# A projection phase in another order: its own PSUM region for queries and for keys, and the moments two images ahead

## What is computed

```
mu = jnp.mean(inputs, axis=-1, keepdims=True)
var = jnp.mean(jnp.square(inputs - mu), axis=-1, keepdims=True)
x = (inputs - mu) / jnp.sqrt(var + LN_EPS) * ln_gamma + ln_beta
q = (x @ Wq + bq).reshape(B, S, H, dh)
k = (x @ Wk + bk).reshape(B, S, H, dh)
v = (x @ Wv + bv).reshape(B, S, H, dh)
```

## Time and profile before

| What | us |
|---|---|
| Median of 3 runs | 4483.35 |
| Lowest and highest of them | 4482.82 and 4495.68 |
| The profiled execution, whole | 4445.29 |
| Its span in the profile | 4443.5 |
| The projection phase in it, first x load to first load of attention | 260.68 |

### The profile page before, as it was taken

One profiled execution on the slowest core, in us unless ns is written; L12 is line 12 of the kernel. 1 busy time (PEld: TensorE's weight loads), 2 busy tenths in 40 slices (PEclk: granted clock), 3 DMA queues, 4 the chain that ended last, 5 costly groups with the idle time before them and its releaser, 6 DMA issues. The chain is left out here.

```text
span 4443.5 us, 74057 instructions
## 1 busy us (share of the span) xinstructions
PE 3361.3 (76%) x26644; PEld 2596.9 (58%) x26644; DVE 2938.2 (66%) x5398; ACT 2246.5 (51%) x3488; POOL 653.8 (15%) x613
## 2 busy tenths in 40 slices
PE   5888888887565888888888888888754447777773
PEld 3665665664453666666666666666544435555552
DVE  7899989986342777777777777777644424444443
ACT  2454445453343766666666666666522224444440
POOL 1000000000110000000000000000077744444441
PEclk9999999999776999999999999999855568888885
DMA  2121322222357999999999999999733234444437
GB/s 78 59 109 66 115 110 79 98 106 106 140 213 239 368 369 358 374 357 374 355 379 352 380 359 358 356 373 373 272 101 128 71 114 156 152 156 154 150 137 303
DMA packets 281139, 988.62 MB, mean 222 GB/s; under 512 B 47796, under 2 KB 53824, under 8 KB 271734
## 3 DMA queue, kind: packets, MB, share of 16 engines
q1 hardware_dynamic: 263542, 950.62, 58.8%
q0 software_dynamic: 17280, 33.87, 2.1%
HBM read 494.69 MB, written 489.85 MB: 222 GB/s over the span
## 5 line engine op out<-in xcount | busy, mean ns | idle before, releaser
L1141 ACT ACTIVATE att_skewed<-att_skewed,att_neg_max 128x1024 f32<-128x1024 f32 x512 | 588.7, 1150 | 438.9 <-DVE att_neg_max L1201 438.9
L1272 PE MATMUL att_turn_ps<-att_ident,att_skewed 128*128 128x128 f32 x4096 | 579.6, 287 | 158.0 <-ACT att_skewed L1141 156.6
L1201 DVE CUSTOM_DVE_ANT_0 att_skewed<-att_score_ps,att_skewed 128x1024 f32<-128x1024 f32 x512 | 626.1, 1223 | 85.5 <-issue 73.5
L1272 PEld LDWEIGHTS att_turn_ps<-att_ident,att_skewed 128*128 128x128 f32 x4096 | 474.7, 146 | 343.0 <-ACT att_skewed L1141 320.5
L1132 ACT ACTIVATE att_rows<-att_wide_ps 128x1152 f32<-128x1152 f32 x512 | 572.8, 1119 | 184.3 <-PE att_wide_ps L1238 183.3
L1209 DVE COPY att_turned<-att_turn_ps 128x1024 f32<-128x1024 f32 x512 | 625.1, 1221 | 20.1 <-PE att_turn_ps L1272 19.4
L1238 PE MATMUL att_wide_ps<-att_ps,att_qs 98*128 98x128 f32 (+3 forms) x1920 | 441.0, 351 | 48.2 <-issue 26.2
L1264 PE MATMUL att_score_ps<-att_ks,att_qs 96*128 96x512 f32 x1024 | 374.7, 448 | 69.5 <-DVE att_neg_max L1201 68.5
L508 ACT ACTIVATE exp_hid<-exp_hid_ps,exp_weights 128x512 f32<-128x512 f32 x284 | 198.0, 697 | 386.9 <-PE exp_hid_ps L587 384.4
L548 DVE CAST exp_hidh<-exp_hid 128x512 fp32r<-128x512 f32 x284 | 126.9, 447 | 386.5 <-ACT exp_hid L508 386.5
L1238 PEld LDWEIGHTS att_wide_ps<-att_ps,att_qs 98*128 98x128 f32 x1920 | 311.1, 201 | 116.4 <-issue 68.1
(11 more groups left out here) (257 smaller groups left out, 5833.9 us busy)
## 6 DMA issues: line engine op xcount, KB each, us to landing
skewed_rows<-att_rows SPq DMA_DIRECT2D x512, 576.0 KB, 7.7
att_skewed<-skewed_rows SPq DMA_DIRECT2D x512, 512.0 KB, 7.8
expert_rows<-conv_pad SPq DMA_DIRECT2D x144, 520.0 KB, 6.9
exp_weights<-split_weights SPq DMA_DIRECT2D x71, 1028.0 KB, 5.0
att_qs<-queries SPq DMA_DIRECT2D x192, 128.0 KB, 7.5
att_ks<-keys SPq DMA_DIRECT2D x192, 128.0 KB, 7.0
exp_rows<-expert_rows SPq DMA_DIRECT2D x71, 260.0 KB, 4.4
sum_part<-expert_parts SPq DMA_DIRECT2D x32, 512.0 KB, 9.6
```

The source lines that it names most:

```text
L1141: act.activation(skewed[r % RING][:], skewed[r % RING][:], ACT.Exp, bias=neg_max[:, k:k + 1], scale=-1.0, accum_out=sums[:, k:k + 1]).then ...
L1201: dve.tensor_tensor_reduce(skewed[r % RING][:], score_ps[:], skewed[r % RING][:], -SCALE, 3.0e38, ALU.add, ALU.min, neg_max[:, k:k + 1]).t ...
L1272: last = pe.transpose(turn_ps[:, t * P:(t + 1) * P], skewed[r % RING][:, t * P:(t + 1) * P], ident[:])
```

## The change

`qk_ps` becomes a list of two regions, one for the queries and one for the keys, and `v_ps` is now another name for `z_ps`: the values of an image are written over its turned tokens, after zh and zl have read them. PE's turn n is channels(n), values(n), project(n, 0), project(n, 1), tokens(n+2), and the lag of one image between channels and products is gone. `channels(n)` waits for the values' copy of image n-1 where it waited for zl(n-1). The products wait for ql and kl of the image before, and the keys no longer for the queries of the same image. DVE's turn is offsets(n+1), zl(n), ql(n), kl(n), moments(n+2). ACT's turn is zh(n), normalise(n+1), the values' copy of n, qh(n), kh(n), and the copy has the wait for the writes of image n-2 too. SP writes the values ahead of the queries.

```diff
--- before.py
+++ after.py
@@ -730,7 +730,8 @@
         rstd, offset = ([sb(f"{s}{b}", [P, TT]) for b in range(2)] for s in ("rstd", "offset"))
         x, xc, vals = pair("x"), pair("xc"), pair("vals")
         zh, zl, qh, ql, kh, kl = (pair(s, F32R) for s in ("zh", "zl", "qh", "ql", "kh", "kl"))
-        token_ps, z_ps, qk_ps, v_ps = psum("token_ps"), psum("z_ps"), psum("qk_ps"), psum("v_ps")
+        token_ps, z_ps, qk_ps = psum("token_ps"), psum("z_ps"), [psum("q_ps"), psum("k_ps")]
+        v_ps = z_ps
 
         loaded, const_set, fold_step, setup_ps, setup_done = (
             sem(s) for s in ("loaded", "const_set", "fold_step", "setup_ps", "setup_done"))
@@ -754,11 +755,11 @@
 
             def keep(n):
                 b = n % 2
+                sp.wait_ge(v_read, n + 1)
+                sp.dma_start(v_dram[n], vals[b][:]).then_inc(kept[b], 16)
                 sp.wait_ge(qk_low, 2 * n + 1)
                 sp.dma_start(q_dram[n, 0], raw(qh[b][:])).then_inc(kept[b], 16)
                 sp.dma_start(q_dram[n, 1], raw(ql[b][:])).then_inc(kept[b], 16)
-                sp.wait_ge(v_read, n + 1)
-                sp.dma_start(v_dram[n], vals[b][:]).then_inc(kept[b], 16)
                 sp.wait_ge(qk_low, 2 * n + 2)
                 sp.dma_start(k_dram[n, 0], raw(kh[b][:])).then_inc(kept[b], 16)
                 sp.dma_start(k_dram[n, 1], raw(kl[b][:])).then_inc(kept[b], 16)
@@ -802,26 +803,23 @@
                 act.wait_ge(qk_filled, 2 * n + j + 1)
                 if j == 0 and n >= 2:
                     act.wait_ge(kept[n % 2], KEPT * (n // 2))
-                act.activation((qh, kh)[j][n % 2][:], qk_ps[:], ACT.Identity, bias=bias[:, j:j + 1]).then_inc(qk_high, 1)
+                act.activation((qh, kh)[j][n % 2][:], qk_ps[j][:], ACT.Identity, bias=bias[:, j:j + 1]).then_inc(qk_high, 1)
 
             def step(n):
                 act.wait_ge(z_filled, n + 1)
                 act.activation(zh[n % 2][:], z_ps[:], ACT.Copy).then_inc(z_high, 1)
                 if n + 1 < NB:
                     normalise(n + 1)
-                if n >= 1:
-                    high(n - 1, 0)
-                    act.wait_ge(v_filled, n)
-                    act.activation(vals[(n - 1) % 2][:], v_ps[:], ACT.Copy).then_inc(v_read, 1)
-                    high(n - 1, 1)
+                act.wait_ge(v_filled, n + 1)
+                if n >= 2:
+                    act.wait_ge(kept[n % 2], KEPT * (n // 2))
+                act.activation(vals[n % 2][:], v_ps[:], ACT.Copy).then_inc(v_read, 1)
+                high(n, 0)
+                high(n, 1)
 
             normalise(0)
             for n in range(NB):
                 step(n)
-            high(NB - 1, 0)
-            act.wait_ge(v_filled, NB)
-            act.activation(vals[(NB - 1) % 2][:], v_ps[:], ACT.Copy).then_inc(v_read, 1)
-            high(NB - 1, 1)
 
         @block.vector
         def _(dve):
@@ -832,7 +830,7 @@
             dve.wait_ge(fold_step, 2)
             dve.tensor_tensor(wl[:], folded[:], raw(wh[:]), ALU.subtract)
             dve.wait_ge(setup_ps, 1)
-            dve.tensor_tensor(bias[:], qk_ps[:, 0:2], vec[:, 2:4], ALU.add).then_inc(fold_step, 1)
+            dve.tensor_tensor(bias[:], qk_ps[0][:, 0:2], vec[:, 2:4], ALU.add).then_inc(fold_step, 1)
             dve.wait_ge(fold_step, 3)
             dve.tensor_tensor(bias[:, 0:1], bias[:, 0:1], vec[:, 4:5], ALU.add).then_inc(setup_done, 1)
             dve.wait_ge(setup_done, 1)
@@ -859,29 +857,27 @@
 
             def low(n, j):
                 dve.wait_ge(qk_high, 2 * n + j + 1)
-                dve.scalar_tensor_tensor((ql, kl)[j][n % 2][:], qk_ps[:], bias[:, j:j + 1], raw((qh, kh)[j][n % 2][:]),
+                dve.scalar_tensor_tensor((ql, kl)[j][n % 2][:], qk_ps[j][:], bias[:, j:j + 1], raw((qh, kh)[j][n % 2][:]),
                                          ALU.add, ALU.subtract).then_inc(qk_low, 1)
 
             moments(0)
             offsets(0)
+            moments(1)
             for n in range(NB):
                 if n + 1 < NB:
-                    moments(n + 1)
+                    offsets(n + 1)
                 dve.wait_ge(z_high, n + 1)
                 dve.tensor_tensor(zl[n % 2][:], z_ps[:], raw(zh[n % 2][:]), ALU.subtract).then_inc(z_low, 1)
-                if n + 1 < NB:
-                    offsets(n + 1)
-                if n >= 1:
-                    low(n - 1, 0)
-                    low(n - 1, 1)
-            low(NB - 1, 0)
-            low(NB - 1, 1)
+                low(n, 0)
+                low(n, 1)
+                if n + 2 < NB:
+                    moments(n + 2)
 
         @block.tensor
         def _(pe):
             pe.wait_ge(loaded, 7 * 16)
             for j in range(2):
-                last = pe.matmul(qk_ps[:, j:j + 1], w[:, j, :], vec[:, 1:2], start=True, stop=True)
+                last = pe.matmul(qk_ps[0][:, j:j + 1], w[:, j, :], vec[:, 1:2], start=True, stop=True)
             last.then_inc(setup_ps, 1)
             pe.wait_ge(setup_done, 1)
 
@@ -896,7 +892,7 @@
             def channels(n):
                 pe.wait_ge(normed, n + 1)
                 if n:
-                    pe.wait_ge(z_low, n)
+                    pe.wait_ge(v_read, n)
                 for t in range(TT):
                     last = pe.transpose(z_ps[:, t * P:(t + 1) * P], xc[n % 2][:, t * P:(t + 1) * P], ident[:])
                 last.then_inc(z_filled, 1)
@@ -905,16 +901,14 @@
                 return ((wh, zh[n % 2]), (wl, zh[n % 2]), (wh, zl[n % 2]))
 
             def project(n, j):
-                if 2 * n + j:
-                    pe.wait_ge(qk_low, 2 * n + j)
+                if n:
+                    pe.wait_ge(qk_low, 2 * n + j - 1)
                 for k, (a, z) in enumerate(terms(n)):
                     for c in (0, HALF):
-                        last = pe.matmul(qk_ps[:, c:c + HALF], a[:, j, :], z[:, c:c + HALF], start=(k == 0), stop=(k == 2))
+                        last = pe.matmul(qk_ps[j][:, c:c + HALF], a[:, j, :], z[:, c:c + HALF], start=(k == 0), stop=(k == 2))
                 last.then_inc(qk_filled, 1)
 
             def values(n):
-                if n:
-                    pe.wait_ge(v_read, n)
                 for t in range(TT):
                     cut = slice(t * P, (t + 1) * P)
                     for k, (a, z) in enumerate(terms(n)):
@@ -923,18 +917,17 @@
 
             def products(n):
                 pe.wait_ge(z_low, n + 1)
+                values(n)
                 project(n, 0)
-                values(n)
                 project(n, 1)
 
             tokens(0)
+            tokens(1)
             for n in range(NB):
-                if n + 1 < NB:
-                    tokens(n + 1)
                 channels(n)
-                if n >= 1:
-                    products(n - 1)
-            products(NB - 1)
+                products(n)
+                if n + 2 < NB:
+                    tokens(n + 2)
 
 
 def attention_phase(nc, NB, x_dram, y_dram, q_dram, k_dram, v_dram, beta, w_qkv, bv, u_bias, v_bias, pos_t, w_out, b_out,
```

## The result

The changed kernel takes 4,521.4 us (median of 6 runs, 4,502.9 to 4,536.5) against 4,483.2 for the kernel before (6 runs, 4,477.9 to 4,495.9). The ratio is 1.0078, 95% interval 1.0048 to 1.0108, so 35 us more, 22 to 48. The forecast was slower by 16 us, 4,499, in a range up to 4,512: the sign was right, the size too small.

What follows compares the result with a forecast made beforehand. A chain of waits bounds the projection phase: 13.85 us plus 2.4 for low clock gives a 16.3 us cycle, +1.1 an image; with the ends about +16 us on 4,483.35, so 4,499, range 4,484 to 4,512.

Steps and rivals of the forecast that it cites:

- the reason given: Projection phase: bursts begin at the low clock with 5.4 us (high level) of work all in the chain; +1.1 us an image.
- The chain at the high level: Projection cycle of one image without low clock: 13.85 us in the new order, 13.95 in the old.
- Rival 2: Projection: clock not low in the chain; cycle 13.9 us, total about -21 us, 4,462 us; chance 0.13.
- the low stretch lasts 2.9 to 6.0 us by the rows ... I take 5.1 us: PE's burst in each projection cycle: time at the low clock, costing 2.4 us, for a cycle of 16.3 us.
- the loss of 0.47 a us: TensorE's matmuls in the projection: of each us at the low level 0.47 is lost.
- The three rows: Profiled low stretches of the kernel before, after PE's idle: 2.9, 5.1 and 6.0 us until the clock rose.
- rival 3: Projection: clock stays low through values, q and k; cycle 18.6 us, total +54 us, 4,537 us; chance 0.07.
- a stretch of transposes: Evidence against a clock staying low through the products: 3.06 us of only transposes in the projection was followed by clock 1.00.
- The ends: Projection's start and finish: zl(0) at 1146.1 instead of 1144.35, kl(15) at 1396.8 instead of 1382.4, then last writes +1.3 us.
- The last cycle: Projection, zl(14) to zl(15): from 1374.3 to 1386.2, forecast 11.9 us.
- the 1.3 us given to writes that come closer together: Projection's end: last writes 1.4 us apart instead of 5.5, costing 1.3 us, between 0 and 2.6.
- ACT's added wait: ACT's new wait for kept ahead of the values' copy in the projection: claimed at no cost.

Runs made afterwards that it cites:

- with the level held: 24 needless 512-column matmuls in PE's idle time of the changed kernel, 20 in the kernel before; ratios 0.9936 and 0.9949, cycles 13.89 and 13.94 us.
- The four replaced bursts: Changed kernel, its 24 value matmuls replaced by 12 of 512 columns, 24 transposes, 24 of 256 columns, or 12 plain f32 products; ratios 1.0007, 1.0025, 1.0007, 1.0018.
- both edits: Changed kernel with zl ahead of offsets and products ordered queries, keys, values, tokens(n+2): ratio 0.9875, phase 213.5 us; with 12 needless matmuls added 0.9862, 198.4 us.
- the changed kernel with filler: Changed kernel with 24 needless 512-column matmuls in PE's idle time before each wait for zl: ratio 0.9936, phase 248.2 us.

## Why the prediction was right and where it failed

The sign was right, and for the reason given. The chain at the high level was right in both orders: 13.85 and 13.95 forecast, 13.89 and 13.94 measured with the level held. So was the reading that the change gains nothing in itself and that the bursts would begin at the low level after more than 5.4 us of idle; PE idles 6.3 to 6.4 us. Rival 2 is out for the kernel as it stands, and right about the cycle (13.9) if the level were held.

The step that failed is the term "the low stretch lasts 2.9 to 6.0 us by the rows ... I take 5.1 us". It lasted 7.1 to 10.5 us. The mechanism was right and this term too small. With the loss of 0.47 a us the stretch that the mean cycle needs is (17.82 - 13.89) / 0.47 = 8.4 us, and the mean of the 14 stretches read from the windows is 8.4. The three rows were of bursts that begin with 512-column products; all 14 of that kind in the kernel before have a mean of 4.3 us, so that 5.1 was long for them and still short of 8.4. I carried their length over to bursts that begin with 128-column rounded products, and gave rival 3 only 0.07 because of a stretch of transposes. The four replaced bursts show that this was the main fault: with another kind of matmul of equal length the cycle is 15.9 to 16.2, inside the forecast's 15.8 to 16.7. The truth lay between forecast and rival 3 (18.6): the level rose while q or k ran. In three of the 14 images it rose only with the end of k, as rival 3 said, and their cycles are 18.7. Over 14 cycles the 1.5 us are 21 of the 23 us by which the phase missed (39.0 against 16).

The ends held: zl(0) came 20.1 us behind the first x load (20.0 forecast). The last cycle was 13.45 against 11.9; its burst was low for 8.7 us, not 5.1. From the last zl to the end of kl it was 11.1 us (10.6 forecast); this last burst began high after 2.8 us of idle and was low for 3.4 us in the middle, which 0.47 a us makes 1.6 us where 1.2 were allowed. From there to the first load of attention it was 5.6 us instead of 4.4, the 1.3 us given to writes that come closer together. ACT's added wait, the x loads, and the order of SP's writes cost nothing that shows: with the level held there is no room for them in 13.89.

Of the Trainium skill's rule (TensorE: Matmul & The Clock Gate, "HAM oscillation — how this bites in real kernels") that bursts between waits start cold each time, the trace agrees for 15 of the 16 bursts of the changed kernel, and not for the last, which began high after 2.8 us of idle; its half of the throttled time would be, as an estimate, 4.2 us an image for the 8.4 us read from the windows; measured 3.9.

## What to carry to other kernels

When a reorder exchanges links of equal length, look at which of them run right after PE's idle: they pay the low level, and the 5.4 us (high level) of matmuls in the chain there cost 3.9 us more here. Put what is not in the chain last in a burst, and put short waits for another engine behind the work that doesn't need them. Where PE idles anyway, needless matmuls can pay: they took 10.5 us out of the phase in the old order, 51 in the changed one and 15 with both edits. The duration of a 128-column matmul at the low level, 0.213 us, carried over from the transposes to the values; the length of the low stretch did not. Ask for rows of the same kind of burst before carrying such a stretch over.

## What the runs showed of the hardware

- Five bursts that last 5.1 us at the low level, each behind 6.4 us of idle: 12 of 512 columns, 24 of 256 columns (both rounded format), 24 transposes and 12 products of 128 columns in plain f32 have cycles of 15.9 to 16.2 us; 24 products of 128 columns in the rounded format, three added up in place each time, have 17.82.
- The level fell at the end of 24 such 128-column products although PE had idled only 0.8 us before them (the second window of the changed kernel with filler).
- A matmul of 128 columns in the rounded format with its load takes 0.213 us low and 0.11 high. At the low level one of 256 columns takes as long (24 in 5.49 us, tail included), so the second 128 columns cost no time.
- A plain f32 product of 128 columns takes twice the time of one in the rounded format and stands in the trace as two (12 of them, 24 records, in 4.37 us, of which the first 3.0 us were low).
